# Expert weights kept in SBUF and addressed by a register on TensorE, smaller records, and gate logits from a split product

## The reference, cut to what matters

```
scores = sigmoid(xf @ gate_w + bias)                       # 2048 tokens x 8 experts
top_scores, top_idx = top_k(scores, 2)
top_scores = top_scores / (sum(top_scores) + 1e-6)
up   = einsum('th,ehi->tei', xf, up_w) + up_b              # 128 -> 512 per expert
hact = gelu(up)
eo   = einsum('tei,eih->teh', hact, down_w) + down_b       # 512 -> 128 per expert
combined = einsum('teh,te->th', eo * 0.1, w)
shared = (gelu(xf @ sw_up + sb_up) @ sw_down + sb_down) * 0.1
out = shared + combined, divided by its largest magnitude per token
```

## Time and profile before

| | us |
|---|---|
| median of 3 runs | 1003.76 |
| lowest and highest of these | 1001.55, 1005.91 |
| profiled execution, whole | 1003.71 |
| profiled execution, span | 1001.7 |
| PE busy in the span | 887.2 |
| mean granted PE clock | 0.943 |

### The profile page before, as it was taken

One profiled execution on the slowest core, in us unless ns is written; L12 is line 12 of the kernel. 1 busy time (PEld: TensorE's weight loads), 2 busy tenths in 40 slices (PEclk: granted clock), 3 DMA queues, 4 the chain that ended last, 5 costly groups with the idle time before them and its releaser, 6 DMA issues. The chain is left out here.

```text
span 1001.7 us, 21092 instructions
## 1 busy us (share of the span) xinstructions
PE 887.2 (89%) x7718; PEld 496.0 (50%) x7718; DVE 702.1 (70%) x1292; ACT 620.9 (62%) x1302; POOL 323.8 (32%) x377
## 2 busy tenths in 40 slices
PE   6399999799999999968888999999999999888980
PEld 4246686556667666734222332222222245778880
DVE  8977747656775586547696789999999944662244
ACT  5424367755554566522388789999989965654542
POOL 1116732135554444512150420000100201673442
PEclk9599999989999999978897999999999998799996
DMA  5029954497875575650210111100010001539982
GB/s 113 1 98 302 150 65 155 167 331 208 256 199 158 158 227 153 161 145 17 88 50 17 42 40 33 33 18 19 19 45 2 2 2 29 183 101 319 321 307 89
DMA packets 71500, 120.80 MB, mean 121 GB/s; under 512 B 16688, under 2 KB 42808, under 8 KB 71208
## 3 DMA queue, kind: packets, MB, share of 16 engines
q1 hardware_dynamic: 64728, 108.44, 37.4%
q0 software_dynamic: 6240, 10.83, 4.0%
q10 hardware_dynamic: 432, 0.20, 0.1%
HBM read 93.61 MB, written 40.55 MB: 134 GB/s over the span
## 5 line engine op out<-in xcount | busy, mean ns | idle before, releaser
L2668 DVE TENSOR_REDUCE front_maxima<-psum 128x1 f32<-128x1024 f32 x240 | 278.5, 1218 | 31.2 <-PE psum L1193 29.9
L2562 ACT ACTIVATE narrow_att_probs<-psum 128x512 f32<-128x512 f32 x512 | 272.7, 598 | 44.1 <-PE psum L2447 38.2
L2461 PE MATMUL psum<-narrow_att_probs,narrow_att_v_ones 128*32 128x256 f32 x2048 | 166.9, 399 | 0.0
L2447 PE MATMUL psum<-narrow_att_q,narrow_att_k 50*128 50x512 bf16 x448 | 142.2, 387 | 10.3 <-ACT narrow_att_probs L2562 10.3
L1193 PE MATMUL psum<-narrow_att_k,narrow_att_q 48*128 48x512 bf16 x448 | 136.4, 385 | 2.9 <-DVE front_maxima L2668 2.2
L2052 DVE TENSOR_REDUCE gated_nmax<-psum 128x1 f32<-128x1024 f32 x62 | 73.0, 1220 | 51.8 <-PE psum L1722 51.5
L1574 POOL DMA_INDIRECT home_rows<-gated_y,gated_to_row x62 | 62.0, 1000 | 136.4 <-ACT gated_y L1792 126.7
L1797 ACT ACTIVATE lead_room<-psum 128x512 f32<-128x512 f32 x62 | 33.7, 594 | 104.5 <-PE psum L1671 104.5
L2461 PEld LDWEIGHTS psum<-narrow_att_probs,narrow_att_v_ones 128*32 128x32 f32 x2048 | 40.9, 109 | 100.1 <-ACT narrow_att_probs L2562 71.7
L1565 POOL DMA_INDIRECT gated_q_rows<-gated_q_dram,gated_from_row x62 | 60.2, 971 | 43.7 <-DVEq L1990 25.5
L3353 ACT ACTIVATE moe_inner<-psum,moe_record 128x128 f32<-128x128 f32 x156 | 44.4, 368 | 45.8 <-PE psum L3266 45.8
(11 more groups left out here) (518 smaller groups left out, 1636.7 us busy)
## 6 DMA issues: line engine op xcount, KB each, us to landing
moe_record<-routed_records SPq DMA_DIRECT2D x39, 578.0 KB, 5.1
gated_k_ring<-gated_k_dram SPq DMA_DIRECT2D x62, 288.0 KB, 4.8
routed_rows<-const_blank SPq DMA_DIRECT2D x12, 792.0 KB, 15.2
lead_room<-gated_v_dram SPq DMA_DIRECT2D x32, 256.0 KB
gated_k_dram<-gated_keys SPq DMA_DIRECT2D x8, 512.0 KB, 5.8
gated_v_dram<-gated_v_stage SPq DMA_DIRECT2D x2, 2048.0 KB, 7.0
lead_wqk_hi<-gated_v_dram SPq DMA_DIRECT2D x16, 256.0 KB
lead_wqk_lo<-gated_v_dram SPq DMA_DIRECT2D x14, 256.0 KB
```

Source lines behind the costliest of these rows:

```text
L2447: pe.matmul(bank, ks(n // 2, kt // QT, e)[rows, tile(kt % QT)], qs(n // 2, n % 2, e)[rows, :], start=True, stop=True, skip_group_check=Tru ...
L2461: last = pe.matmul(psum[32 * j:32 * j + 32, SUM_BANK, cols], v_ones[:, n // 2 % 2, kt, j, :], probs[:, (n * STILES + kt) % 3, j, cols], st ...
L2562: act.activation(probs[:, k % 3, 2 * e + u % 2, :], psum[:, SCORE_BANK + j % 3, :], ACT.Exp, scale=SCALE).then_inc(exped, 1)
L2668: dve.tensor_reduce(maxima[:, n % 2, at:at + 1], chunk.rearrange("p a b -> p (a b)"), AX.X, ALU.max, negate=True).then_inc(chunk_used, 1)
```

## The change

Eight down weight matrices are loaded once into SBUF (`weights`, 128 x 8 x 512 floats) at the start of the experts phase. `down_chunk` takes its moving operand from there at an address made from a register of PE, which PE loads from `places` in four groups of 9 or 10 experts. The record keeps up weights and biases (644 floats per partition, 322 KB). Record and entry of a chunk now share a ring of 8, a semaphore and one reading of the registers, and the record waits for what the entry waited for. `fill` no longer copies down weights. The gate logits of a batch come from six float32r products of 512 columns, with the gate columns, split into a high and a low part, as stationary operand; the gate columns of the second quarter stand at another 32 columns of a zeroed tile, so one bank holds both quarters of a batch, experts along partitions. ACT takes the exponential with the bias in it over 64x512, and PE turns the result back in four transposes (`turn_gates`), which `choose` reads. In the narrow attention phase `turn_gates` stands at the step of `project_next`, two steps behind `gates`; in the experts phase behind down of quarter 0.

```diff
@@ fill
         for e in range(E):
-            sp.dma_start(self.records[e, :, HID:2 * HID]..., io["L1_ffn_down_w"][e]...).then_inc(self.records_ready, 16)
-            sp.dma_start(self.records[e, :, 2 * HID:2 * HID + D], ...)
+            sp.dma_start(self.records[e, :, HID:HID + D], ...)
@@ Back.load
+        sp.wait_ge(self.tables_ready, 4)
-            sp.dma_start(self.gate_w[:, :], io["L1_ffn_gate_w"])...
-            sp.dma_start(self.gate_row[0:1, :, :], ...)
+            for x in range(2):
+                sp.dma_start(self.gate_w[:, x, 32 * x:32 * x + E], io["L1_ffn_gate_w"])...
+                sp.dma_start(self.gate_bias[32 * x:32 * x + E, :], ...)
@@ Back.split
+        pool.tensor_scalar(self.gate_neg[:, :], self.gate_bias[:, :], -1.0, None, ALU.mult)...
+        pool.tensor_copy(self.gate_hi[:, :, :], self.gate_w[:, :, :])...
+        pool.wait_ge(self.weights_split, 2)
+        pool.tensor_tensor(self.gate_lo[:, :, :], self.gate_w[:, :, :], f32(self.gate_hi[:, :, :]), ALU.subtract)...
@@ logits, raise_gates, turn_gates, choose
-        pe.matmul(bank[:, 0:STILES * self.E], self.one_row..., self.gate_row..., start=True, ...)
-        for s, part in enumerate((high, low)):
-            for t in range(STILES):
-                last = pe.matmul(bank[:, t * self.E:(t + 1) * self.E], f32(part(t)), self.gate_w[:, :], ...)
+        for x in range(PERB):
+            last = split_product(pe, bank[0:64, :], self.gate_hi[:, x, :], self.gate_lo[:, x, :], high[:, quarter(x)], low[:, quarter(x)],
+                                 start=(x == 0), stop=(x == PERB - 1))
-        act.activation(self.scores..., bank[:, 0:STILES * self.E], ACT.Exp, scale=-1.0)
+        act.activation(self.logits_t, bank[0:64, :], ACT.Exp, bias=self.gate_neg[:, 0:1], scale=-1.0)
+    def turn_gates(self, pe, b, bank, ident):
+        pe.wait_ge(self.gate_stage, self.TURNED * b + self.RAISED)
+        for i in range(PER_Q):
+            last = pe.transpose(bank[:, 64 * i:64 * i + 64], self.logits_t[:, tile(i)], ident[0:64, 0:64])
+        last.then_inc(self.gate_stage, 1)
-        dve.tensor_scalar(self.scores, self.scores, 1.0, self.LARGEST, ALU.add, ALU.min)
+        dve.tensor_scalar(self.scores..., turned, 1.0, self.LARGEST, ALU.add, ALU.min)     # turned: a view of the bank
@@ experts_phase, SP
-                if j >= RECORDS:
-                    sp.wait_ge(y_ready, j - RECORDS + 1)
-                sp.reg_load(regs, back.places[0:1, j, :])
-                sp.dma_start(record[:, j % RECORDS, :], ...).then_inc(record_loaded[j % RECORDS], 16)
+            for e in range(E):
+                sp.dma_start(weights[:, e, :]..., io["L1_ffn_down_w"][e]...).then_inc(experts_loaded, 16)
+            for j in range(CHUNKS):      # load_entry(j):
                 if j >= ENTRIES:
                     routed.wait_returned(sp, j % ENTRIES, j // ENTRIES)
                 sp.reg_load(regs, back.places[0:1, j, :])
+                sp.dma_start(record[:, j % ENTRIES, :], ...).then_inc(entry_loaded[j % ENTRIES], 16)
                 sp.dma_start(entry[:, j % ENTRIES, :], ...).then_inc(entry_loaded[j % ENTRIES], 16)
@@ experts_phase, PE
-                    last = pe.matmul(..., inner[:, j % 2, a, :], record[:, j % RECORDS, HID + a * D:HID + (a + 1) * D], ...)
+                    last = pe.matmul(..., inner[:, j % 2, a, :], weight(j, a * D), ...)
+            def load_experts(g):
+                pe.wait_ge(back.table_step, back.EARLY_STEPS + (back.LATE_STEPS if g else 0))
+                at, to = GROUPS[g:g + 2]
+                pe.reg_load(regs[g % 2][0:to - at], back.places[0:1, at:to, 0])
+            def weight(j, at):
+                g = max(n for n in range(len(GROUPS) - 1) if GROUPS[n] <= j)
+                e = pe.snap(regs[g % 2][j - GROUPS[g]], min_val=0, max_val=E - 1)
+                return weights[:, bass.ds(e, 1), at:at + D].rearrange("p e n -> p (e n)")
             down(0)
+            back.turn_gates(pe, 1, psum[:, CHAIN_BANK, :], C["ident"])
             up(2, blocks[:2])
+            load_experts(0)              # behind turn_back, ahead of turn_entry(0)
+            pe.wait_ge(experts_loaded, 16 * E)    # ahead of up_chunk(0)
+                if j and j in GROUPS:    # ahead of down_chunk(j), j = 9, 19, 29
+                    load_experts(GROUPS.index(j))
```

More of the change, by code:

```diff
@@ L2392, in gates, with turn_gates @@
                     freed(number[("back", "rows")])
-                    back.logits(pe, psum[:, i % 2 * 2, :], lambda t: UH[:, tile(t)], lambda t: UL[:, tile(t)])
+                    back.logits(pe, psum[:, i % 2 * 2, :], UH, UL)
+                def turn_gates():
+                    back.turn_gates(pe, 0, psum[:, number[("back", "gates")] % 2 * 2, :], C["ident"])
                 def positions():
@@ L2498, in _ @@
                         if at == BACK_AT["project_next"]:
+                            turn_gates()
                             project_next()
@@ L2627, in add_next @@
                 def add_next(i):
-                    back.choose(dve, 0)
+                    back.choose(dve, 0, psum[:, (i + 1) % 2 * 2, :])
                     dve.wait_ge(chunk_done, i + 1)
@@ L2702, in __init__ @@
         self.fb = self.hid // P
-        self.record = 2 * self.hid + D + self.fb
+        self.record = self.hid + D + self.fb
         self.rows = nc.dram_tensor("routed_rows", [self.ROWS, self.WIDTH], F32, kind="Internal").ap()
@@ L2715 @@
     BLANKS = ROWS // (BLANK * P)
-    RECORD_LOADS = 1 + 3 * E
+    RECORD_LOADS = 1 + 2 * E
     def fill(self, sp):
@@ L2894, with choose @@
     LARGEST, BEYOND = 1e30, 2e30
-    def choose(self, dve, b):
-        step = self.step[b]
+    def choose(self, dve, b, bank):
+        step, PERB = self.step[b], QUARTERS // BATCH
         dve.wait_ge(self.small_loaded, 16 * self.SMALL)
-        dve.wait_ge(self.raised, b + 1)
-        dve.tensor_scalar(self.scores, self.scores, 1.0, self.LARGEST, ALU.add, ALU.min).then_inc(step, 1)
+        dve.wait_ge(self.gate_stage, self.TURNED * (b + 1))
+        turned = bank[:, 0:64 * PER_Q].rearrange("p (i x s) -> p x i s", i=PER_Q, x=PERB)[:, :, :, 0:self.E]
+        dve.tensor_scalar(self.scores.rearrange("p (x i) e -> p x i e", x=PERB), turned, 1.0, self.LARGEST, ALU.add, ALU.min).then_inc(step, 1)
         dve.wait_ge(step, 1)
@@ L3056, in experts_phase @@
         shared = ph.sb("shared", [P, TILES, D])
-        record = ph.sb("record", [P, RECORDS, routed.record])
+        weights = ph.sb("weights", [P, E, HID])
+        record = ph.sb("record", [P, ENTRIES, routed.record])
         entry = ph.sb("entry", [P, ENTRIES, WIDTH])
@@ L3080, in experts_phase @@
         acc_turned, shared_ready = ph.sem("acc_turned"), ph.sem("shared_ready")
-        record_loaded = [ph.sem(f"record_loaded{s}") for s in range(RECORDS)]
+        experts_loaded = ph.sem("experts_loaded")
         entry_loaded = [ph.sem(f"entry_loaded{s}") for s in range(ENTRIES)]
@@ L3216, in logits @@
                 pe.wait_ge(rows_low, PERB)
-                back.logits(pe, psum[:, CHAIN_BANK, :], lambda t: UH[:, tile(t)], lambda t: UL[:, tile(t)])
+                back.logits(pe, psum[:, CHAIN_BANK, :], UH, UL)
             def up(q, blocks):
@@ L3265, in up_chunk @@
                 for a in range(FB):
-                    last = pe.matmul(psum[:, INNER_BANK[j % 3], tile(a)], record[:, j % RECORDS, tile(a)], entry_t[:, j % 2, :],
+                    last = pe.matmul(psum[:, INNER_BANK[j % 3], tile(a)], record[:, j % ENTRIES, tile(a)], entry_t[:, j % 2, :],
                                      start=True, stop=True, skip_group_check=True)
@@ L3276, in down_chunk @@
                     pe.wait_ge(inner_ready, j * FB + a + 1)
-                    last = pe.matmul(psum[:, OUTER_BANK[j % 2], 0:D], inner[:, j % 2, a, :], record[:, j % RECORDS, HID + a * D:HID + (a + 1) * D],
+                    last = pe.matmul(psum[:, OUTER_BANK[j % 2], 0:D], inner[:, j % 2, a, :], weight(j, a * D),
                                      start=(a == 0), stop=(a == FB - 1), skip_group_check=True)
                 last.then_inc(outer_done, 1)
+            regs = [[pe.alloc_register(f"expert{s}_{n}") for n in range(GROUP)] for s in range(2)]
+            GROUPS = [0] + list(range(Routed.EARLY, CHUNKS, GROUP)) + [CHUNKS]
+            def load_experts(g):
[6 more added lines that the diff above has]
+                return weights[:, bass.ds(e, 1), at:at + D].rearrange("p e n -> p (e n)")
             blocks = range(FB)
@@ L3431, in _ @@
             low_parts(0)
-            back.choose(dve, 1)
+            back.choose(dve, 1, psum[:, CHAIN_BANK, :])
             take_shared(0)
```

73 lines of the change are left out of this document (32 added, 41 removed).

## The result

| | before | after |
|---|---|---|
| median of the runs | 1002.65 (4 runs, 1001.14 to 1005.91) | 989.02 (4 runs, 987.56 to 991.19) |
| ratio, 95% interval | | 0.987 [0.984, 0.990] |
| profiled execution, whole and span | 1003.71, 1001.7 | 987.56, 985.7 |
| mean granted PE clock | 0.943 | 0.952 |

Forecast 989.5, measured 989.0. The sum was right and several of its terms were not. Batch 0's stage gave about twice what was forecast; the register loads took over three times theirs; a stand behind the loads of batch 0's results, which the forecast counted among what leaves the loop, stayed; the register arithmetic cost nothing. These nearly cancel.

What follows compares the result with a forecast made beforehand. The prediction saw three places that count: the chunk loop, held by DMA and SP's issuing, and the gate logits of batches 0 and 1. Sum: 1003.7 - 3.7 - 2.0 - 8.5 = 989.5 us, range 981 to 1002.

Steps and rivals of the forecast that it cites:

- Step 1: Batch 0's gate logits in the narrow attention: fewer matmuls and a clock that stays up, -3.7 us.
- the clock term: Behind batch 0's logits: dense products keep PE's clock up, 2.0 us gained, between bounds of 0 and 2.9.
- The wait at `turn_gates`: Batch 0, PE waiting for ACT's longer exponential: 0 to 0.6 us, taken as 0.3.
- Step 2: Batch 1's gate logits in the experts phase: down 1 starts earlier, -2.0 us, bounds 0.5 and 2.6.
- step 4: Costs that come in with the chunk loop's change: ring 1 us, register operations 3, four register readings 2.
- Step 3: Chunk loop: smaller records and fewer SP register readings put both DMA limits below PE, worth up to 14.5 us.
- the floor of 76 us: Chunk loop: 39 chunks of 1.90 us, 74.1, plus about 2.0 that remains whatever the weights do.
- Step 4a: Chunk loop: the record waits for the scatter 8 chunks before; cycle 7.2 to 11.1 us, covered, 1 us for hiccups.
- Step 4b: PE's register work for each down matmul in the chunk loop: 0.08 us a chunk, 3 us.
- Rival A: Slower: register work binds PE in `down_chunk`, 1013 us at full cost; sign turns at 0.44 us a chunk; chance 0.12.
- Step 4c: PE's four readings of 9 or 10 registers: 0.47 to 2.4 us each, taken as 0.5 each, 2 us.
- Step 5: Shorter `fill` at the start, and small loads and POOL instructions in the narrow attention: counted at nothing.

Runs made afterwards that it cites:

- e5: The changed kernel run again, unchanged: 989.74 us, 0.985 of the kernel before.
- e1: The kernel before with only the gate half of the change, down weights still coming with the records: 991.65 us, 0.986.
- e12: The kernel before run again, unchanged: 1003.75 us, 1.001.
- e11: e4 with batch 0's results brought home in four loads of 256 KB, behind entries 30, 32, 34 and 36: 981.43 us, 0.979.
- e4: The changed kernel with one register loaded on PE ahead of each chunk's down product, in place of four grouped loads: 984.22 us, 0.977.
- e9: The changed kernel, grouped register loads kept, with the second home load behind entry 34 instead of 30: 989.21 us, 0.986.
- e6: e4 with four registers loaded ahead of each chunk's down product, one of them used: 992.03 us, 0.986.
- e3: The changed kernel with the eight copies of down weights still made at the start, into a table nobody reads: 991.72 us, 0.985.
- e2: The kernel before with only the weights, records and register half of the change, gates as before: 1002.31 us, 0.998.
- e7: e4 with the second home load of batch 0's results behind entry 34 instead of 30: 981.20 us, 0.976.

## Why the prediction was right, and where it wasn't

**Step 1, batch 0 (-3.7): right in kind, the clock term far too small.** The logits fell from 4.03 to 1.54 us and 0.5 for the transposes, the 2.0 of the sum. The wait at `turn_gates` taken at 0.3 was 0. The clock's term had the upper bound 2.9, from the one fall that the one profile of before showed; four profiles with the old logits show stages of 20.65 to 26.72 us. At full clock they would hold 15.5 + 2.0 = 17.5, so the falls cost 3.1, 4.7, 4.8 and 9.2 us, 5.4 in the mean. None of the nine with the new logits shows a fall there. The whole step is worth 5.1 us against the profile that was read, 7.5 us against the mean of the four. That the sparse logits are the cause was left open between 0 and 2.9; that they are is borne out by the table, four profiles against nine (which of their traits does it, the 8 columns or the number of instructions, was not tried). How far the clock falls after them is different each time; what sets that no run here shows.

**Step 2, batch 1 (-2.0): right in kind, its size not settled.** PE stands 2.50 us before `positions` (2.9 forecast), `choose` starts 3.5 us after the logits' end (3.5 to 4), the clock falls behind the stand (0.42 us a product until 857, some 1.2 us lost; at most 1.5 was allowed; in e5 it doesn't fall). Up to the loop it is 2.2 us less than in before, with a register load in it that the prediction had booked in step 4. But this stretch holds other falls of the clock: e1, which has no such load, takes 40.52 us there, and before and e12 take 42.58 and 40.99.

**Step 3, what leaves the loop (14.5): right in kind, too large.** DMA share 0.64 for 0.85, 185 GB/s for 283; PE's 9.3 us of waits for records are gone, pairs are issued as close as 1.55 us apart (1.42 forecast; 2.06 in the earlier trace rows). But the floor of 76 us is too low by 4.3, for the best loop is 80.3 (e11). Of its 38 intervals 3.23 and 2.34 are the table steps, 1.8 us together for the 1.5 in the sum; the three late intervals ahead of the home loads hold 2.7, those behind them about 1. The text gave the whole 14.5 us to the DMA share and to SP's 2.06 us a chunk. 3.3 of it was one stand, the 5.23 us interval behind the home loads, and that one stays.

**Step 4a, the ring (1 us): right as asked, wrong in what was asked.** Scatters land in 3.4 us and records in 3.1, by which the cycle is 8.6 us, in the lower half as forecast, and no wait comes from the ring by itself until entry 31. (Where PE is quicker, as in e4 and e11, some do: up to 1.3 us at one chunk.) But the text looked only at the cycle of scatter and pair and not at what else SP issues between pairs. Two home loads of 512 KB go out behind entry 30, the DMA share is 1.03 at 371 GB/s, an entry comes 1.95 us late, and the clock halves behind it: 4.4 us (7.6 - 4.8 + 3.1 - 1.9 + 0.4, from e9), for the 1 us in the sum. The kernel before pays about the same at this place, 3.3 us in one profile and 7.4 in the other. So this is less a cost of the change than a part of the 14.5 that never was to be had.

**Step 4b, register operations (3 us): wrong, they cost nothing where the loads are short.** 156 of 63 ns, two MOVEs' worth each; dense chunks are 1.90 us as without them. Rival A, 0.44 us a chunk from which the sign turns, is nowhere near: after leaves 0.79 us of the sequencer free in each chunk. e6 shows that the mechanism is real all the same, with 1.02 us of load.

The Trainium skill's figure of about 62 ns of sequencer for each MATMUL with hardware decode off ("TensorE: Matmul & The Clock Gate", section "Wait — 56ns, not 53.3ns?") does not fit e6. No run here shows how decode is set. By that figure, as an estimate, 17 matmuls a chunk (x312 + x312 + x39 over 39 chunks; the prediction counted 18) would be 1.05 us, with register operations and load 2.32, and the interval is 2.13. What is left there for a matmul and its weight load together is at most 0.86 / 17 = 51 ns.

**Step 4c, four readings of registers (2 us): this is the term that failed.** It was taken at 0.5 us each from the one row of its kind, a load of two values on SP; its upper end, 2.4 us from the same row times the number of values, is what they took to the tenth. The prediction wrote down both ends and chose by nearness to a row instead of by the number of values in it. The runs make it a line: 0.305 us for 1 register, 0.477 for 2 (SP), 1.02 for 4, 2.42 for 9 or 10, which is 0.24 a register. PE stood 1.61 us for the one ahead of the loop, 1.60 and 1.64 for the next two (2.42 less the 0.79 that a chunk hides) and 2.34 for the last, 7.2 us for the 2 in the sum (6.6 if the 1.61 counts as the 1.0 that e4 got back). The last fell beside the late entry and did not hide behind it: PE waited 1.95 us for the entry and then 2.34 for the load, because the load sits in the same in-order queue behind the entry's transpose.

The Trainium skill has this price: about 200 ns a register, even for bulk ("Runtime: NRT & Kernel Launch", section "Instruction fetch mechanics"). By it the four loads would be an estimated 7.8 us (39 registers); the prediction didn't use it. That page speaks of loads from HBM; here they come from SBUF, and the runs show 0.24 us a register.

**Step 5, at nothing: right.** e3 has the copies back and is neither later in the phases that follow nor slower.

**The sum.** Forecast -3.7 - 2.0 - 8.5 = -14.2. In the means of two profiles each: -8.2, -1.6, -3.7 = -13.5. The forecast's 989.5 owes its closeness to luck: an underestimate of 4.5 us in step 1 and an overestimate of 4.8 us in the loop. A reader who had only the result would have taken the loop for the source, as did the prediction; e1 and e2 say that it is the gates.

**The faster version.** e7 (981.2) and e11 (981.4) beat both kernels: 2.1 to 2.4% below before, where the change as made is 1.3 to 1.5%. What lies between are the register loads: e4, which changes them alone, has 0.977 already, against 0.976 of e7. What the home loads' places add can't be told from these times.

## What to carry to other kernels

A load of registers from memory is priced by the register, and here PE's queue hid only what the array's work left free in one iteration: load one per iteration just ahead of its use, not ten every tenth. Before all the time above a floor is put down to one limit, look at the largest single waits and at what else the same queue issued just ahead of each: here the one behind the two home loads, an interval of 5.23 us, stayed when the records got smaller. And where a stretch of tiny matmuls precedes a fall of the granted clock, take the clock from several executions, as one profile shows only one draw: replacing them was worth twice their own time here.

## What the hardware showed that was not expected

- PE's TENSOR_LOAD takes 0.305 us for one register and 0.24 us for each further one; the register arithmetic for an address takes 63 ns and cost nothing that shows, except in e6, if its sequencer binds.
- With the sparse logits (34 matmuls, 8 columns each but two) the stage took 20.65 to 26.72 us for the same instructions, at a clock of 0.83 to 0.62; with dense ones 15.51 us in nine profiles out of nine.
- The phases before the first logit ended at 818.1 to 824.2 us in thirteen profiles, in no order that follows the edits. A difference of 5 us there between two single profiles is no evidence for an edit.
